# Decoder layer on one core: key weights of batches 3 to 15 formed one head pair at a time for a group of batches, and kept in DRAM

## What is computed

```python
kv = context @ Wkv.T
k, v = jnp.split(kv, 2, axis=-1)          # 64 context tokens per batch, 16 heads x 64
sim = jnp.einsum('bhid,bhjd->bhij', q, k) * SCALE     # q = x @ Wq.T
attn = jax.nn.softmax(sim, axis=-1)
out = jnp.einsum('bhij,bhjd->bhid', attn, v)
```

## Time and profile before

| | us |
|---|---|
| median of 3 runs (1277.67 to 1278.22) | 1277.95 |
| the profiled execution | 1278.95 |
| its span, first to last instruction | 1277.2 |
| TensorE busy in the span | 1240.4 (97%) |
| VectorE, ScalarE, GpSimd busy | 874.9, 570.2, 632.2 |
| share of TensorE in the chain that ended last | 87% |

### The profile page before, as it was taken

One profiled execution on the slowest core, in us unless ns is written; L12 is line 12 of the kernel. 1 busy time (PEld: TensorE's weight loads), 2 busy tenths in 40 slices (PEclk: granted clock), 3 DMA queues, 4 the chain that ended last, 5 costly groups with the idle time before them and its releaser, 6 DMA issues.

```text
span 1277.2 us, 22575 instructions
## 1 busy us (share of the span) xinstructions
PE 1240.4 (97%) x8080; PEld 1123.7 (88%) x8080; DVE 874.9 (69%) x1696; ACT 570.2 (45%) x1119; POOL 632.2 (50%) x986
## 2 busy tenths in 40 slices
PE   8968999999999999999999999998999999999998
PEld 7857999999999999999999999887798899899888
DVE  5536988888889888888888898887534323323335
ACT  2124546555555465555655554654524313412420
POOL 3215756767667567576675675665422112112201
PEclk9979999999999999999999999999999999999999
DMA  9831111011111021111111111140140111011001
GB/s 278 200 74 34 35 34 54 26 55 43 34 50 51 26 59 34 43 42 35 51 49 34 51 42 34 39 124 22 34 132 14 55 66 67 1 67 67 1 1 34
DMA packets 117475, 69.98 MB, mean 55 GB/s; under 512 B 74099, under 2 KB 114804, under 8 KB 117365
## 3 DMA queue, kind: packets, MB, share of 16 engines
q1 hardware_dynamic: 115332, 67.87, 18.2%
q10 hardware_dynamic: 2032, 0.66, 0.2%
HBM read 42.29 MB, written 26.22 MB: 54 GB/s over the span
## 4 chain that ended last, share of the span: by engine, by line
PE 87%; DVE 4%; POOL 1%; issue 1%; ACT 1%; POOLq 0%; DVEq 0%
PE ob L137 7%; PE ob L138 7%; PE ob L139 7%; PE sim L137 7%; PE sim L138 7%; PE sim L139 7%; PE pw L417 4%; PE pt L466 4%; PE pw L137 3%; PE pw L138 3%; PE pw L139 3%; PE pw L369 3%; PE pt L138 2%; PE pt L139 2%; PE pt L137 2%; PE pw L393 2%
## 5 line engine op out<-in xcount | busy, mean ns | idle before, releaser
L1513 POOL TENSOR_TENSOR w_lo<-w_raw,w_hi 128x2048 fp32r<-128x2048 f32 x16 | 73.8, 4614 | 222.7 <-ACT w_hi L1453 169.6
L137 PE MATMUL ob<-b_hi,pT_hi 128*128 128x256 f32 x512 | 153.0, 299 | 3.8 <-DVE pT_lo L822 3.8
L139 PE MATMUL ob<-b_hi,pT_lo 128*128 128x256 f32 x512 | 144.7, 283 | 0.0
L138 PE MATMUL ob<-b_lo,pT_hi 128*128 128x256 f32 x512 | 144.6, 282 | 0.0
L902 POOL TENSOR_TENSOR prob<-prob,rz 128x512 f32<-128x512 f32 x128 | 131.1, 1045 | 11.5 <-DVE rz L769 11.5
L684 ACT ACTIVATE prob<-prob 128x512 f32<-128x512 f32 x128 | 80.8, 632 | 112.5 <-DVE prob L815 111.7
L810 DVE TENSOR_REDUCE mx<-sim 128x8 f32<-128x512 f32 x128 | 87.9, 687 | 37.4 <-PE sim L139 36.1
L596 ACT ACTIVATE x<-h,nmr,rstd 128x256 f32<-128x256 f32 x128 | 76.3, 596 | 64.2 <-POOL nmr L836 59.2
L137 PEld LDWEIGHTS ob<-b_hi,pT_hi 128*128 128x128 f32 x512 | 97.3, 190 | 8.5 <-DVE pT_lo L822 7.8
L137 PE MATMUL sim<-a_hi,tT_hi 128*128 128x512 f32 x256 | 104.2, 407 | 0.0
L829 POOL TENSOR_SCALAR ve<-mv 128x1 f32<-128x1 f32 x128 | 28.1, 219 | 148.9 <-DVE mv L732 147.5
(11 more groups left out here) (241 smaller groups left out, 3871.6 us busy)
## 6 DMA issues: line engine op xcount, KB each, us to landing
xraw<-in_x SPq DMA_DIRECT2D x16, 512.0 KB, 4.0
kv_scratch<-stage SPq DMA_DIRECT2D x32, 256.0 KB, 2.8
x_scratch<-x SPq DMA_DIRECT2D x64, 128.0 KB, 1.7
out_x<-o_sb SPq DMA_DIRECT2D x64, 128.0 KB, 1.7
w_raw<-in_L_ffn_experts_inter SPq DMA_DIRECT2D x8, 1024.0 KB, 5.0
w_raw<-in_L_ffn_experts_out SPq DMA_DIRECT2D x8, 1024.0 KB, 7.7
kraw<-kv_scratch SPq DMA_DIRECT2D x32, 128.0 KB, 2.9
vraw<-kv_scratch SPq DMA_DIRECT2D x32, 128.0 KB, 3.1
```

The lines of the kernel that those rows point to most:

```text
L137: pe.matmul(out, lh, rh, start=first, stop=False)
L138: pe.matmul(out, lh, rl, start=False, stop=False)
L139: return pe.matmul(out, ll, rh, start=False, stop=last)
```

## The change

Batches 0, 1 and 2 get their A as before, but all before tile 0: pieces A in iteration -2, C (batch 1) and D (batch 2) in iteration -1. C and D go through a staging tile to a new DRAM tensor `a_scratch`. Batches 3 to 8 and 9 to 15 form two groups. For each of the 8 head pairs and each group there is a unit: keys of this pair for 6 or 7 batches side by side. 16 units in all, each in a slot of `UNIT_SLOTS`, with four pieces U_0 to U_3 (two heads, two halves of the channels). The 64 contracted channels of one head fill only half of the array's 128 rows, so both parts of the operand split are stacked: the keys' high part on rows 0 to 63, the low part on rows 64 to 127, Wq's high part twice, Wq's low part twice. A piece is two fp32r products of 384 or 448 columns. SP loads keys and Wq twice into SBUF (`load_unit`), ScalarE and POOL make the parts (`act_stack`, `pool_stack`, in the slots of `STACK_SLOTS`), ScalarE copies each piece to `a_stage`, SP stores it (112 and 15 partitions for the channels with the mask row, 128 for the others). In slot 3 of every batch SP loads the next batch's whole A into `a_lo`, one half as soon as sim of that half has read the old one; ScalarE rounds it to `a_hi`, VectorE subtracts in place. The mask rows are written to `a_scratch` in the setup, by 15 small stores. Keys have a DRAM layout of their own with 2 KB per partition. The order of steps within a slot is new on all engines: among others z follows directly on the transposes, the norm of x1 on ScalarE comes after the first preps, the output norms come after the copy of `tr`, and POOL's `v_lo` comes before the other work of slot 3.

```diff
-    kv_scr = nc.dram_tensor("kv_scratch", (2, NB, P, PAIRS, NKV), F32).ap()
+    k_scr = nc.dram_tensor("k_scratch", (PAIRS, P, NB * NKV), F32).ap()
+    v_scr = nc.dram_tensor("v_scratch", (NB, P, PAIRS, NKV), F32).ap()
+    w_scr = nc.dram_tensor("w_scratch", (PAIRS, P, C), F32).ap()
+    a_scr = nc.dram_tensor("a_scratch", (NB, P, MC, KEYS), F32).ap()
...
+    GROUPS = (slice(OLD, 9), slice(9, NB))
...
+    UNIT_SLOTS = (0, 1, 3, 4, 5, 7, 8, 9, 12, 15, 16, 19, 20, 23, 27, 31)
+    STACK_SLOTS = (0, 1, 2, 4, 5, 6, 8, 9, 12, 13, 16, 17, 20, 21, 25, 29)
...
-        "A1": ((3, 1), (3, 0), (3, 2)), "A0": ((3, 1), (3, 1), (3, 3)),
...
+        "A0": ((0, 8), (0, 10), (0, 9)), "A1": ((2, 4), (1, 13), (1, 9)),
...
+        if name[0] == "A":
+            return it == -2
+        if name[0] in "CD":
+            return it == -1
+        if name[0] == "U":
+            return TPB * it + int(name[1]) in UNITS
...
     def sp_slot(sp, it, slot, e):
...
+        if early_pieces(n):
+            store_unit(sp, n, 0)
+        if slot == 3 and it >= 0 and within(it + 1):
+
+            for h in range(2):
+                sp.wait_ge(s["sim_made"], 2 * n + h + 1)
+                if it + 1 < OLD:
+                    sp.wait_ge(s["rows_stored"], 16 * sum(STORES) * (it + 1))
+                else:
+                    for m in range(MC):
+                        sp.wait_ge(s[f"a_stored{m}"], 16 * STORES[m] * PAIRS * (1 if it + 1 < GROUPS[0].stop else 2))
+                sp.dma_start(f32(half(a_lo, h)), a_scr[it + 1, :, :, h * HK:(h + 1) * HK]).then_inc(s[f"a_loaded{h}"], 16)
+        if early_pieces(n):
+            store_unit(sp, n, 1)
...
+        if n == -1:
+
+            prep_done(sp, -1, last_of("D0", "D1", "D2", "D3"))
+            store_rows(sp, 2)
+            sp.wait_ge(s["rows_stored"], 16 * 2 * sum(STORES))
+            load_unit(sp, 0)
+        for u in stacked_in(n):
+            if u + 1 < 2 * PAIRS:
+                sp.wait_ge(s["stack_made"], u + 1)
+                load_unit(sp, u + 1)
+        if n in UNITS and not early_pieces(n):
+            store_unit(sp, n, 0)
+            store_unit(sp, n, 1)
...
+        return (slice(16, P), slice(1, 16)) if m == 0 else (slice(0, P),)
...
+    def store_unit(sp, n, m):
+
+        prep_done(sp, n // TPB, last_of(*pieces_of(n)[2 * m:2 * m + 2]))
+        u = UNITS[n]
+        bs, r = batches_of(u), u % PAIRS
+        for p in rows_of(m):
+            sp.dma_start(a_scr[bs, p, m, r * P:(r + 1) * P].rearrange("b p j -> p b j"),
+                         a_stage[p, m, 0:bs.stop - bs.start, :, :].rearrange("p b e j -> p b (e j)")
+                         ).then_inc(s[f"a_stored{m}"], 16)
+
+    def load_unit(sp, u):
...
+        for q in (slice(0, 64), slice(64, P)):
+            sp.dma_start(k_twice[q, :, 0:width], k_scr[r, :, c].rearrange("(e p) j -> p e j", e=2)).then_inc(s["r_loaded"], 16)
+        for q in (slice(0, 64), slice(64, P)):
+            sp.dma_start(w_twice[q, :, :], w_scr[r, :, :].rearrange("(e p) c -> p e c", e=2)
+                         ).then_inc(s["w_loaded"], 16)
...
+            pe.wait_ge(s["stack_made"], u + 1)
+            c = slice(m * P, (m + 1) * P)
+            pe.matmul(pw[:, g], w_stack_hi[:, e, c], k_stack[:, e, g], start=True, stop=False)
+            last = pe.matmul(pw[:, g], w_stack_lo[:, e, c], k_stack[:, e, g], start=False, stop=True)
...
         elif slot == 0:
-            prep_done(pe, it - 1, last_of("A2", "A3"))
+            pe.wait_ge(s["a_ready"], 2 * (it - 1) + h + 1)
...
+    def act_stack(act, u):
+
+        act.wait_ge(s["r_loaded"], 32 * (u + 1))
+        if u:
+            n = UNIT_SLOTS[u - 1]
+            act.wait_ge(s["prep_made"], number(n // TPB, last_of(*pieces_of(n))))
+        g = slice(0, (batches_of(u).stop - batches_of(u).start) * NKV)
+        act.activation(k_stack[:, :, g], k_twice[:, :, g], ACT.Copy)
+        act.wait_ge(s["w_loaded"], 32 * (u + 1))
+        act.activation(w_stack_hi[:, :, :], w_twice[:, :, :], ACT.Copy).then_inc(s["stack_hi"], 1)
...
+        act.activation(half(a_hi, h), f32(half(a_lo, h)), ACT.Copy).then_inc(s["a_hi_made"], 1)
...
+        dve.tensor_tensor(half(a_lo, h), f32(half(a_lo, h)), f32(half(a_hi, h)), ALU.subtract).then_inc(s["a_ready"], 1)
...
+    def pool_stack(pool, u):
+
+        pool.wait_ge(s["stack_hi"], u + 1)
+        lo, g = slice(64, P), slice(0, (batches_of(u).stop - batches_of(u).start) * NKV)
+        pool.tensor_tensor(w_stack_lo[:, :, :], w_twice[:, :, :], f32(w_stack_hi[:, :, :]), ALU.subtract
+                           ).then_inc(s["w_lo_made"], 1)
+        pool.wait_ge(s["w_lo_made"], u + 1)
+        pool.tensor_tensor(k_stack[lo, :, g], k_twice[lo, :, g], f32(k_stack[lo, :, g]), ALU.subtract
+                           ).then_inc(s["stack_made"], 1)
+        pool.wait_ge(s["stack_made"], u + 1)
...
+                for b in range(1, NB):
+                    sp.dma_start(a_scr[b, 0:1, 0, :].rearrange("p (g j) -> p g j", j=NKV),
+                                 maskrow[:, b * NKV:(b + 1) * NKV].unsqueeze(1).broadcast_to([1, 2 * PAIRS, NKV])
+                                 ).then_inc(mask_stored, 16)
```

More of the change, by code:

```diff
@@ L529, in pe_slot @@
         prep(3)
+        if tail_tile(it, slot) is not None:
+            ff["pe_up"](pe, 0, tail_tile(it, slot))
+        prep(4)
         if has_x1T or has_xT:
             pe_tr(pe, n, it + 2, slot, par(1 if slot else 0), par(0), has_x1T, has_xT)
-        prep(4)
+        if has_z:
+            pe_z(pe, it, slot)
+        prep(6)
         if (it, slot) == (NB - 1, 1):
@@ L757, in dve_slot @@
             dve_max(dve, n, 1)
+        prep(4)
         if has_sim:
             dve_shift(dve, n, q, 1)
-        prep(5)
         if has_prev:
             dve_pT(dve, n - 1, 0)
+        prep(6)
+        if has_z:
+            need(dve, "z_made", n + 5)
+            dve_stats(dve, 0, n + 4, q, zb[:, :].rearrange("p (a c) -> p a c", c=P)[:, 0:4:3, :])
+        if has_x1T or has_xT:
+            need(dve, "tr_hi", n + 9)
+            hi, lo, src = tr_views(slot, has_x1T, has_xT)
+            dve.tensor_tensor(lo, src, f32(hi), ALU.subtract).then_inc(s["tr_taken"], 1)
+        prep(8)
         if has_sim:
@@ L802, in dve_slot @@
             dve_stats(dve, 1, n + 4, q, h1[:, q, :])
+        if (it, slot) == (NB - 1, 3):
+            ff["dve_small"](dve)
+        prep(17)
+        if loads_a(it, slot):
+            dve_a(dve, it + 1, 1)
+        if tail_tile(it, slot) is not None:
+            ff["dve_up"](dve, 0, tail_tile(it, slot) + 1)
+        prep(19)
     def by_head(ap):
@@ L884, in pool_slot @@
             pool_rstd_twice(pool, n - 2, q)
+        if slot == 3 and within(it + 1):
+            need(pool, "v_hi_made", it + 2)
+            pool.tensor_tensor(v_lo[:, :, :], vraw[:, :, :], f32(v_hi[:, :, :]), ALU.subtract).then_inc(s["v_lo_made"], 1)
+        for u in stacked_in(n):
+            pool_stack(pool, u)
         if slot == SPLIT_SLOT and within(it + 2) and not (isinstance(it, int) and it == -2):
@@ L892, in pool_slot @@
             pool.tensor_tensor(x1_tile, x1_tile, boutbc[:, :], ALU.add).then_inc(s["x1_biased"], 1)
-        if slot == 3 and within(it + 1):
-            need(pool, "v_hi_made", it + 2)
-            pool.tensor_tensor(v_lo[:, :, :], vraw[:, :, :], f32(v_hi[:, :, :]), ALU.subtract).then_inc(s["v_lo_made"], 1)
-        if has_z:
-            pool_rstd(pool, 0, n + 4, q)
         if has_sim:
@@ L912, in pool_slot @@
             ff["pool_small"](pool)
-        if (it, slot) == (NB - 1, 0):
-            ff["pool_weights"](pool, 0, 0, 0)
-    FIRST_PREPS = [n for n in NAMES if enabled(n, -2) and n[0] != "Q"]
+    FIRST_PREPS = [n for n in NAMES if enabled(n, -2) and n[0] not in "AQ"]
     def first_prep(eng, kind, i):
@@ L1151, in _ @@
                     load_wkv(3)
+                if n == 2 * PAIRS + RING:
+                    sp.wait_ge(padded, 2)
+                    for i in range(RING):
+                        sp.wait_ge(staged[i], 16 * (2 * PAIRS // RING))
+                    load_k(sp, 0)
                 if n == 14:
```

248 lines of the change are left out of this document (160 added, 88 removed), and 26 rows, old and new, of the table ORDER.

## The result

The changed kernel takes 1281.25 us in the median of 20 runs (1278.33 to 1285.64), the kernel before, timed beside it, 1278.26 in 20 runs (1277.20 to 1279.75). The ratio is 1.0026 with a 95% interval of 1.0019 to 1.0032: **slower by 0.26%, 3.0 us**, where 24 us less were forecast, a range of 1246 to 1267. The profiled execution took 1282.62 us, its span is 1280.5.

The account below looks back on a forecast made before the run. In the 64 tiles the time was taken as the sum of TensorE's work. -20.8 (TensorE's net) - 7.5 (A forward) + 3 (first unit) + 1.5 (other units) = -23.8 on 1278.95 gave 1255.2, as median 1254 us; range 1246 to 1267.

Parts of the forecast that it names:

- TensorE's net, -20.8: 13 batches: A's groups removed, 45.4 us off TensorE; 128 unit products added, 24.6 us; bounds -16 to -23.6.
- A loaded: Slot 3: both halves of A loaded behind sim's last use, 4.0 us each, priced at nothing since TensorE has other work.
- if the cover is gone: Case for the load of A: without other TensorE work to hide it, each us late costs 15 us in all.
- TensorE waiting for `a_lo` at slot 0: Sign that the forecast is wrong: TensorE waits for the loaded key weights' low part at the start of slot 0.
- The other units, +1.5: Slots with units: stacking on ScalarE and POOL and SP's DMAs make pieces or probabilities late, +1.5 us (0 to 6).
- Edits at nothing: Mask stores (5 us of SP in the setup, 0.34 us each), added DMA traffic and early `v_lo`, all priced at nothing.
- A late setup: Sign that the forecast is wrong: the setup ends late.
- A moved forward: A of batches 0 to 2 goes to iterations -2 and -1, partly filling TensorE's idle time: -7.5 us (-12 to 0).
- the first unit: Loads and stack behind D's last copy take 11 to 12 us, TensorE has about 8 of other work: +3 (0 to 8).
- VectorE sets the pace: Rival, chance 0.15: in iterations 8 to 14 VectorE, 93% of 47.0 us, holds the period at 48.7; 1266 us.
- The products cost as f32: Rival, chance 0.02: the units' fp32r products take twice the distance, as f32 does, adding 24.6 us; 1278 us.
- Each unit late: slower: Rival, chance 0.07: SP loads each unit behind the output's store, ScalarE waits; 1294 at 2.5 us each, 1318 at 4.

Follow-up runs that it names:

- e11: e10 with, in slot 1, TensorE's B2 piece moved behind the first group of transposes of the probabilities: 1259.03 us, 0.9856 of the kernel before.
- e6: Changed kernel with SP's two loads of the next batch's key weights ahead of the stores of the unit's pieces in slot 3: 1274.69 us, ratio 0.9980.
- e10: e9 with ST's products in slot 2 placed between z and the second group of transposes of the probabilities: 1259.07 us, 0.9855 of the kernel before.
- e9: Changed kernel with the edits of e1 and e6 together: 1267.17 us, 0.9920 of the kernel before.
- e12: e9 with POOL's stack subtractions cut to 4 columns for units 1 to 15 (not the wanted layer): 1265.37 us, ratio 0.9909.
- e1: Changed kernel with the 15 mask stores replaced by one DRAM to DRAM transfer in iteration -1: 1274.44 us, 0.9971 of the kernel before.
- e3: Changed kernel with POOL's stack subtractions cut to 4 columns for units 1 to 15 (not the wanted layer): 1280.43 us, ratio 1.0009.
- e5: Changed kernel with TensorE's order altered in slots 1 (a piece of B) and 2 (ST's products) to stand behind z: 1285.08 us, ratio 1.0053.

## Why the prediction was wrong

**TensorE's net, -20.8: right.** Two units of 448 columns each take 3.33 us of distances in iteration 5, 1.67 each, against 0.205 x 8 = 1.64. A's groups are gone, and e11's late period is the forecast one within 0.04 us. The expected gain was there in TensorE's work; it was given back in waits.

**"A loaded: I cost it at nothing": the step that failed in the loop.** I let the load start at sim's last use. The diff in the document shows `store_unit` ahead of it in SP's list, and that store waits for ScalarE. I asked how long the load takes, not what stands ahead of it in its queue. The load was also slower than I took it, 5.9 us in the median where the x loads had 4.0 (in the window with units DMAs moved 73 GB/s more than before, where I had added 40), but with it first in the queue no wait for `a_lo` was left in iterations 2 to 5 of e6: what stood ahead of it decided. It cost 7.4 us of the loop (e6), near what "if the cover is gone" would have priced at 1 us for each batch with units. TensorE waiting for `a_lo` at slot 0 was the sign that I had named.

**The order in a slot: the step that was missing.** The sum took each batch as distances of products, as if the places between them did not matter. Slot 2 cost 6.6 us in the loop (e10 against e9), slot 1 a net 0.9 (e11 against e10), and the tail's 2.5 us short fits two more such batches (2 x 0.96 = 1.9): in e11 the tail is 495.2, 7.4 below before's, with 7.0 forecast.

**"The other units, +1.5": too small.** After the two mends and the order, e11's loop is 11.5 us below before's, 7.8 short of -19.3. POOL's stacks are 1.8 of it (e12, measured on e9), where I had looked for trouble. In e11's trace TensorE's waits of over 0.05 us in iterations 0 to 7 add up to 6.9 us, 2.6 of them in iteration 0 with its three units; the largest part, 2.9, is for `b_lo` behind ScalarE's stack copies, which was not tried by itself. So no single cause is shown for this term.

**"Edits at nothing", the mask stores: wrong, +5.1 us.** 15 at 0.34 were 15 at 0.63, and "TensorE runs without a gap" hides nothing once the queue that frees its stage buffers is full. The slack to compare them with was SP's 5.3 us. "A late setup" was a sign that I had named. What put the changed kernel's setup later already ahead of the stores, 2.9 us in the two profiles, stays open; it is near the spread of 2.8 us that kernels with one and the same list show there.

**A moved forward and the first unit: better than forecast.** -2.9 where +2.5 stood. C and D filled idle time, and the second of two stretches at the lower clock is gone. The first stays (0.50 from 76 to 82 us before, from 77.1 to 83.8 after). From 90 to 100 us the granted clock was 0.69 before, with TensorE busy 6.71 us; after, it is

```profile
90.00:100.00 10.00, 9.02 (x62) 8.07 (x60) 3.52 (x8) 4.94 (x10) 2.54 (x6) 1.00 0.12 27
```

**The rivals.** "VectorE sets the pace" had the right engine in part and the wrong mechanism: VectorE's `pT_lo` and `a_lo` end last at single places, and its subtraction and POOL do hold each other up (2085 and 2035 ns), but TensorE's order decided: with VectorE's work unchanged the late period fell to 47.1. "The products cost as f32" came nearest to the measured time by chance; the products cost what was forecast (1.67 us a unit). Its "twice" was misread besides: in the earlier trace rows eight f32 products of 128 columns take 1.70 us, 0.21 each, against 0.18 for 384 columns of fp32r, so 3.5 times a column. "Each unit late: slower", the one that ended on the right side, was not the mechanism: the units' own products wait 0.15 to 0.18 us for their stack, in three of six units from iteration 3 to 5. The slower result came from three losses, 6.8, 6.6 and 8.1 us by the medians of e1, e6 and e10, all at something that I had set at nothing or not set down.

## What to carry to other kernels

Where a change moves work off the bounding engine, list for each place that it empties what stood there as cover for a wait, above all between two uses of one PSUM bank. For each new transfer read the queue's list ahead of it: a store that waits for an engine delays the load behind it, and many tiny stores cost the queue's time for each, not by bytes. A loss in one place can eat a mend in another (e3, e5), so take the latest link of a chain first, and test the mends together.

## What was not expected of the hardware

- A store of one partition with a broadcast source, 4 KB, holds SP's queue 0.63 us (15 in 9.41 us), nearly twice the 0.34 of `out_x` with 128 KB. One transfer from DRAM to DRAM with all 15 rows took 0.93 us of the queue in e1.
- A one-input pass of VectorE at 657 ns for 1024 columns and POOL's product stretch each other (to 1546 and 1495 ns); `tensor_reduce` over the same columns is not stretched in any of 64 (1206 to 1221 ns), 60 of which run beside POOL.
- The loads of x, 512 KB, the same as before, went from 4.0 us to 7.5 in the median, with 43 GB/s turned to 116 from 300 to 400 us. From iteration 0 on they are issued 0.6 to 1.4 us behind a load of A. The last one ahead of the first such load, at 113.5 us, still took 3.3; from 578 us on, with 59 GB/s in all, the others take 6.1 to 7.5. So their place behind the loads of A counts more than the traffic in the mean. The page's last part, after:

```profile
a_lo<-a_scratch SPq DMA_DIRECT2D x30, 512.0 KB, 5.9
xraw<-in_x SPq DMA_DIRECT2D x16, 512.0 KB, 7.5
```
